# Two more parts of layer 0 in high and low halves, held in rings of four, with the parts placed mostly in tile 1 and the sum over d ahead of tile 1's half sum

## The reference, cut to what is computed

```python
e = jnp.stack([tbl_0[ids[:, 0]], ..., tbl_38[ids[:, 38]]], axis=1)      # (512, 39, 16)
x0 = xk = e
for W in (f0, f1, f2):                      # f0: (39*39, 128), f1 and f2: (128*39, 128)
    z = jnp.einsum('bfd,bgd->bfgd', x0, xk).reshape(b, f * g, d)
    cur = jnp.einsum('bpd,pm->bmd', z, W)
    outs.append(cur); xk = cur
z = jnp.sum(jnp.concatenate(outs, axis=1), axis=-1)                      # (512, 384)
h = relu(concat([z, dense_ctx]) @ W_top1 + b_top1)
h = relu(h @ W_top2 + b_top2)
y = h @ W_top3
```

## Time and profile before

| | us |
|---|---|
| median of 3 runs | 701.53 |
| the profiled execution | 700.51 |
| its span | 698.7 |
| around the span | 1.8 |

### The profile page before, as it was taken

The page is one execution under the profiler, slowest core; times in us unless marked ns, Lnnn a source line. Parts: engine busy times, 40 slices in busy tenths (PEclk is TensorE's granted clock), DMA queues, the critical chain, the costliest instruction groups (busy, mean ns, idle before and its releaser), DMA issues. The chain is left out here.

```text
span 698.7 us, 11739 instructions
## 1 busy us (share of the span) xinstructions
PE 643.2 (92%) x2567; PEld 472.3 (68%) x2567; DVE 538.7 (77%) x1216; ACT 518.5 (74%) x1842; POOL 429.9 (62%) x416
## 2 busy tenths in 40 slices
PE   0578999999999999999999999999999999999988
PEld 0246777676767677777777676767676777776663
DVE  1426788888887979797988888888979797999880
ACT  1226688788797878787887888787878787888862
POOL 6876568686767676767678686767676534101330
PEclk9877999999999999999999999999999999999999
DMA  7551332231304040313131221313040320301000
GB/s 206 117 118 30 88 74 45 45 72 37 80 10 106 9 107 3 85 31 77 39 77 40 56 61 39 77 23 93 9 108 4 96 63 0 109 0 44 29 1 0
DMA packets 58221, 40.28 MB, mean 58 GB/s; under 512 B 36626, under 2 KB 41056, under 8 KB 58203
## 3 DMA queue, kind: packets, MB, share of 16 engines
q1 hardware_dynamic: 52376, 38.73, 22.1%
q0 software_dynamic: 5120, 1.29, 2.4%
q10 hardware_dynamic: 706, 0.06, 0.1%
HBM read 38.13 MB, written 1.94 MB: 57 GB/s over the span
## 5 line engine op out<-in xcount | busy, mean ns | idle before, releaser
L640 ACT ACTIVATE parts<-psa,x0c 128x128 f32<-128x128 f32 x1536 | 440.7, 431 | 94.6 <-PE psa L793 88.2
L532 DVE SCALAR_TENSOR_TENSOR parts<-psd,x0c,parts 128x128 f32<-128x128 f32 x960 | 266.0, 342 | 80.9 <-PE psd L793 64.1
L503 DVE TENSOR_REDUCE cur<-parts 128x64 f32<-128x1536 f32 x128 | 223.6, 1747 | 23.7 <-ACT parts L640 18.8
L789 PE MATMUL psa<-w1h,x1h 128*128 128x512 f32 x384 | 175.3, 457 | 5.9 <-issue 5.9
L793 PE MATMUL psa<-w1h,x1l 128*128 128x512 f32 x384 | 152.4, 397 | 0.0
L790 PE MATMUL psa<-w1l,x1h 128*128 128x512 f32 x384 | 152.2, 396 | 0.0
L359 POOL TENSOR_TENSOR z0l<-pairs,z0h 117x512 fp32r<-117x512 f32 x56 | 72.7, 1298 | 122.6 <-ACT z0h L596 122.4
L343 POOL DMA_INDIRECT emb<-tables,idx x130 | 126.7, 975 | 23.3 <-issue 19.8
L352 POOL TENSOR_TENSOR pairs<-x0t,pairs 117x512 f32<-117x512 f32 (+1 forms) x105 | 135.1, 1296 | 7.3 <-DMA x0t<-x_rows 6.6
L789 PE MATMUL psd<-w1h,x1h 128*128 128x512 f32 (+1 forms) x256 | 115.2, 450 | 12.1 <-DVE parts L532 12.1
L793 PE MATMUL psd<-w1h,x1l 128*128 128x512 f32 (+1 forms) x256 | 97.8, 382 | 0.0
(11 more groups left out here) (83 smaller groups left out, 524.5 us busy)
## 6 DMA issues: line engine op xcount, KB each, us to landing
pairs<-x_rows SPq DMA_DIRECT2D x113, 156.0 KB
pairs<-x_rows SPq DMA_DIRECT2D x30, 234.0 KB
x0t<-x_rows SPq DMA_DIRECT2D x16, 234.0 KB
emb<-tables,idx POOLq DMA_INDIRECT x130
x_rows<-emb SPq DMA_DIRECT2D x13, 72.0 KB
wt_sb<-w_top SPq DMA_DIRECT2D x1, 768.0 KB, 5.9
parts<-w SPq DMA_DIRECT2D x1, 704.0 KB, 4.9
x_rows<-emb SPq DMA_DIRECT2D x13, 40.0 KB
```

The costliest lines, as they stand in the source:

```text
L503: return dve.tensor_reduce(cur1[:, t % 2, first:end], terms[:, first:end, :, :], AX.XY, ALU.add)
L532: op = dve.scalar_tensor_tensor(acc, y[:, M * j:M * j + M], x0c[:, t, GF * g + j:GF * g + j + 1], acc, ALU.mult, ALU.add)
L640: op = act.activation(lanes(dst, j), y[:, M * j:M * j + M], ACT.Copy, scale=x0c[:, t, GF * g + j:GF * g + j + 1])
L789: pe.matmul(y[:, 0:n], hi, w1h[:, c], start=True, stop=False)
```

## The change

Parts 0 and 1 join `SPLIT`, which is now 0 to 5; only part 6 stays in plain f32 and now closes the sum. `z0h` and `z0l` stay four slots large and become rings, so parts 4 and 5 take the slots of 0 and 1 once PE is through with these. The tables of all engines are new for every block but the first, and `SUM_AT` goes from tile 2 to the end of tile 1; `SCALARS_AT`, `ZH_AT` and `ZH_EARLY_AT` have no version of their own for block 0. POOL makes low parts 0 and 1 behind gather 8, and gather 9 goes ahead of low part 2.

```diff
-L0_AT = {(0, 5): 0, (0, 7): 1, (0, 9): 2, (1, 1): 3, (1, 3): 4, (1, 5): 6, (1, 8): 5}
-L0_AT_FIRST = {(1, 6): 0, (1, 8): 1, (2, 0): 2, (2, 2): 3, (2, 4): 4, (2, 6): 6, (2, 8): 5}
+L0_AT = {(0, 6): [0], (1, 0): [1], (1, 1): [2], (1, 3): [3], (1, 4): [4], (1, 8): [5], (1, 9): [6]}
+L0_AT_FIRST = {(1, 6): [0], (1, 8): [1], (2, 0): [2], (2, 2): [3], (2, 4): [4], (2, 6): [5], (2, 8): [6]}
...
-SPLIT = [2, 3, 4, 5]
-L0_END = 5
+SPLIT = [0, 1, 2, 3, 4, 5]
+L0_END = 6
 NS = len(SPLIT)
-ZH_AT = {(0, 2): 3, (0, 4): 4, (1, 1): 5}
-ZH_EARLY_AT = {(3, 4): 2}
+HIGHS, LOWS = 4, 4
+ZH_AT = {(0, 0): 3, (1, 0): 4, (1, 2): 5}
+ZH_EARLY_AT = {(2, 5): 0, (3, 0): 1, (3, 5): 2}
...
-SUM_AT, SUM_AT_FIRST = (2, 2), (3, 0)
-HIGH_AT = {(2, 4): 0, (3, 0): 1, (3, 2): 2}
+SUM_AT = (1, 3)
+SUM_AT_FIRST = (3, 0)
+HIGH_AT = {(2, 0): 0, (2, 3): 1, (3, 3): 2}
-LOW_AT = {(2, 3): 0, (3, 0): 1, (3, 1): 2}
+LOW_AT = {(2, 0): 0, (2, 3): 1, (3, 3): 2}
-SCALARS_AT = {(2, 2): 0, (2, 3): 1, (3, 1): 2}
+SCALARS_AT = {(1, 2): 0, (2, 0): 1, (3, 5): 2}
...
+        def high_slot(i):
+            return z0h[0:ROWS, COLS * (i % HIGHS):COLS * (i % HIGHS) + COLS]
...
                 pool.wait_ge(z0h_ready, (b - 2) * NS + i + 1)
+                pool.wait_ge(l0_steps, L0T * b + (SPLIT[i - LOWS] + 1 if i >= LOWS else 0))
...
                 if ahead2:
+                    pair_low_part(b + 2, 0)
+                    pair_low_part(b + 2, 1)
+                if gather_ahead:
+                    gather(9)
+                if ahead2:
                     pair_low_part(b + 2, 2)
-                if gather_ahead:
-                    gather(9)
...
-                act.wait_ge(l0_steps, L0T * b)
+                act.wait_ge(l0_steps, L0T * b + (SPLIT[i - HIGHS] + 1 if i >= HIGHS else 0))
...
-                    pe.matmul(ps0[:, :], w0h[0:ROWS, w], z0h[0:ROWS, c], start=False, stop=False)
+                    pe.matmul(ps0[:, :], w0h[0:ROWS, w], high_slot(i), start=(k == 0), stop=False)
```

More of the change, by code:

```diff
@@ L58 @@
 assert all(p.count("a") == SLOTS and p.count("d") <= SLOTS for p in PATTERN)
-L0_AT = {(0, 5): 0, (0, 7): 1, (0, 9): 2, (1, 1): 3, (1, 3): 4, (1, 5): 6, (1, 8): 5}
-L0_AT_FIRST = {(1, 6): 0, (1, 8): 1, (2, 0): 2, (2, 2): 3, (2, 4): 4, (2, 6): 6, (2, 8): 5}
-TURN_AT, TURN_AT_FIRST = (0, 8), (1, 5)
+L0_AT = {(0, 6): [0], (1, 0): [1], (1, 1): [2], (1, 3): [3], (1, 4): [4], (1, 8): [5], (1, 9): [6]}
+L0_AT_FIRST = {(1, 6): [0], (1, 8): [1], (2, 0): [2], (2, 2): [3], (2, 4): [4], (2, 6): [5], (2, 8): [6]}
+TURN_AT = (0, 8)
+TURN_AT_FIRST = (1, 5)
 WARMING = 3
-SPLIT = [2, 3, 4, 5]
-L0_END = 5
+SPLIT = [0, 1, 2, 3, 4, 5]
+L0_END = 6
 NS = len(SPLIT)
-ZH_AT = {(0, 2): 3, (0, 4): 4, (1, 1): 5}
-ZH_EARLY_AT = {(3, 4): 2}
+HIGHS, LOWS = 4, 4
+ZH_AT = {(0, 0): 3, (1, 0): 4, (1, 2): 5}
+ZH_EARLY_AT = {(2, 5): 0, (3, 0): 1, (3, 5): 2}
 assert sorted([*ZH_AT.values(), *ZH_EARLY_AT.values()]) == SPLIT
-SUM_AT, SUM_AT_FIRST = (2, 2), (3, 0)
-HIGH_AT = {(2, 4): 0, (3, 0): 1, (3, 2): 2}
+SUM_AT = (1, 3)
+SUM_AT_FIRST = (3, 0)
+HIGH_AT = {(2, 0): 0, (2, 3): 1, (3, 3): 2}
 HIGH_AT_FIRST = {(3, 2): 0, (3, 3): 1, (3, 5): 2}
-LOW_AT = {(2, 3): 0, (3, 0): 1, (3, 1): 2}
+LOW_AT = {(2, 0): 0, (2, 3): 1, (3, 3): 2}
 LOW_AT_FIRST = {(3, 1): 0, (3, 2): 1, (3, 3): 2}
-SCALARS_AT = {(2, 2): 0, (2, 3): 1, (3, 1): 2}
+SCALARS_AT = {(1, 2): 0, (2, 0): 1, (3, 5): 2}
 PIECES = [(0, 2), (2, 4), (4, L0T)]
@@ L148, in build @@
         pairs = sb("pairs", [128, L0T, COLS])
-        z0h = sb("z0h", [128, NS * COLS], F32R)
-        z0l = sb("z0l", [128, NS * COLS], F32R)
+        z0h = sb("z0h", [128, HIGHS * COLS], F32R)
+        z0l = sb("z0l", [128, LOWS * COLS], F32R)
         x1h = sb("x1h", [128, COLS], F32R)
@@ L172, in build, with low_slot @@
         y_sb = s0[0:1, :]
+        def high_slot(i):
+            return z0h[0:ROWS, COLS * (i % HIGHS):COLS * (i % HIGHS) + COLS]
+        def low_slot(i):
+            return z0l[0:ROWS, COLS * (i % LOWS):COLS * (i % LOWS) + COLS]
         def lanes(w, j):
@@ L357, in pair_low_part @@
                 pool.wait_ge(z0h_ready, (b - 2) * NS + i + 1)
-                c = slice(COLS * i, COLS * i + COLS)
-                pool.tensor_tensor(z0l[0:ROWS, c], pairs[0:ROWS, k, :], z0h[0:ROWS, c].bitcast(F32),
+                pool.wait_ge(l0_steps, L0T * b + (SPLIT[i - LOWS] + 1 if i >= LOWS else 0))
+                pool.tensor_tensor(low_slot(i), pairs[0:ROWS, k, :], high_slot(i).bitcast(F32),
                                    ALU.subtract).then_inc(z0l_ready, 1)
@@ L390, in first_block @@
                 gather_early(0, 9)
+                pair_low_part(2, 0)
+                pair_low_part(2, 1)
                 pair_low_part(2, 2)
@@ L438, in block_of @@
                 if ahead2:
-                    pair_low_part(b + 2, 2)
+                    pair_low_part(b + 2, 0)
+                    pair_low_part(b + 2, 1)
                 if gather_ahead:
                     gather(9)
+                if ahead2:
+                    pair_low_part(b + 2, 2)
             pool.wait_ge(ids_in, 16)
@@ L593, in pair_high_part @@
                 act.wait_ge(z0_ready, (b - 1) * L0T + k + 1)
-                act.wait_ge(l0_steps, L0T * b)
-                c = slice(COLS * i, COLS * i + COLS)
-                act.activation(z0h[0:ROWS, c], pairs[0:ROWS, k, :], ACT.Copy).then_inc(z0h_ready, 1)
+                act.wait_ge(l0_steps, L0T * b + (SPLIT[i - HIGHS] + 1 if i >= HIGHS else 0))
+                act.activation(high_slot(i), pairs[0:ROWS, k, :], ACT.Copy).then_inc(z0h_ready, 1)
             def high_part(b, t):
@@ L739, in layer0 @@
                     pe.wait_ge(z0l_ready, (b - 2) * NS + i + 1)
-                    c = slice(COLS * i, COLS * i + COLS)
                     w = slice(M * i, M * i + M)
-                    pe.matmul(ps0[:, :], w0h[0:ROWS, w], z0h[0:ROWS, c], start=False, stop=False)
-                    pe.matmul(ps0[:, :], w0h[0:ROWS, w], z0l[0:ROWS, c], start=False, stop=False)
-                    pe.matmul(ps0[:, :], w0l[0:ROWS, w], z0h[0:ROWS, c], start=False, stop=(k == L0_END)).then_inc(l0_steps, 1)
+                    pe.matmul(ps0[:, :], w0h[0:ROWS, w], high_slot(i), start=(k == 0), stop=False)
+                    pe.matmul(ps0[:, :], w0h[0:ROWS, w], low_slot(i), start=False, stop=False)
+                    pe.matmul(ps0[:, :], w0l[0:ROWS, w], high_slot(i), start=False, stop=(k == L0_END)).then_inc(l0_steps, 1)
                     return
@@ L795, in block_of @@
                             l0_at = L0_AT_FIRST if starts(b) else L0_AT
-                            if (t, g) in l0_at:
-                                layer0(b + 1, l0_at[t, g])
+                            for k in l0_at.get((t, g), []):
+                                layer0(b + 1, k)
                             if (t, g) == (TURN_AT_FIRST if starts(b) else TURN_AT):
@@ L809, in _ @@
             turn_x0(0)
-            for k in [*(k for k in range(L0T) if k != L0_END), L0_END]:
+            for k in range(L0T):
                 layer0(0, k)
```

## The result

The changed kernel takes 668.80 us, the median of four runs (666.62 to 670.97), against 701.25 of the kernel before in four runs on the same chip. The ratio is 0.9533, its interval 0.9494 to 0.9572, so 32.45 us are gone. The profiled execution took 669.16 us with a span of 667.3; in the two spans it is 31.4. Lines move: the groups of layer 1 are now L801, L802 and L805, the halves of a part L754 to L756, the part in f32 L759, the turn of x0 L770, `grams` L779, the half sum L517, the sum over d L511, x1l L507, DVE's products L546, ACT's products L653, x1h L624, the high part L609, the low part L368.

A forecast was written before the change was run, and what follows sets the result against it. PE was taken as the path, stalled by late DVE: A and B 18.6, C 9.1, parts 4.5, ends 0.9, less 1.0 residual stall, make 32.1 us; span 698.7 to 666.6, median 669.4, forecast 669, range 664 to 684.

The forecast's parts named there:

- A: PE's stall ahead of group 6 of tile 3, for a bank of DVE: 0.54 us a block, to go.
- B: PE's stall ahead of group 9 of tile 3, for a bank of DVE: 0.79 us a block, to go.
- C: PE's stall ahead of part 0 of the next block, for x1l: 0.70 us in 13 blocks, to go.
- The margins of 0.02 and 0.07: Time by which group 4's bank is free before group 9 needs it: 0.02 in tile 3, 0.07 in tile 2.
- ACT's idle 0.75: ACT's x1h of tile 0 waits 0.75 us for the sum over d, making DVE's half sum of tile 2 late.
- Parts, 0.16 each: Parts 0 and 1 in halves instead of f32 save PE 0.16 us each, 28 times: 4.5 us.
- The ends: Block 1's wait for x1l and block 15's stall: 0.9 us taken from both, between 0 and 2.
- Block 1's wait for x1l: PE's longest wait for x1l, 1.0 us, said to move a group back.
- The bound of 1.7 for block 0: In block 0 ACT may wait for the turn of x0 at (1, 2): nothing taken, 1.7 us at most.
- Rivals 2 and 3: POOL bounds: 690, chance 0.08; PE waits for z0l at (1, 4) and (1, 8): 715, chance 0.05.
- Rival 1: DVE stays late, so B stays at 0.3 to 1.0 us a block: 679, chance 0.19.
- Rival 4: Stalls only move to tile 2 or tile 0 and the parts alone are saved: 697, chance 0.06.

The follow-up runs named there:

- the DVE experiment: Changed kernel plus three sums over one input (tensor_reduce) on DVE behind the second half sum in tile 3: 672.34 us, ratio 0.972.
- the control: The changed kernel itself, unedited, run again on the third chip beside the third group of experiments: 660.41 us, ratio 0.9555.
- the first group: The first of three groups of follow-up runs, edits of the changed kernel; the kernel before took 700.62 us there.
- the other two groups: The second and third groups of follow-up runs, each on another chip; the kernel before took 691.93 and 691.17 us there.

## Why the prediction was right

It said 669, a gain of 32.1 and a block of 35.0; measured were 668.8, 32.4 (31.4 in the spans) and 35.04. That 669 was met to 0.2 is luck: the span came out 0.7 longer than the sum, and the median, put 1.0 above the profiled run, lay 0.4 below it; the two misses cancel. The block is the better test. Point by point:

- **PE is the path.** Right. Of the 37.30 us of the block before, 2.03 were A, B and C and 35.27 slots of matmuls; now PE is busy in all of a block, and each added stall of PE came out in the time: 0.50 in the DVE experiment made the block 0.50 longer.
- **A and B, 1.33 a block.** Right in size. The half sum of tile 2 was put at 0.64 into tile 3 and came at 0.71, the one of tile 3 at 0.83 into tile 0 and came at 1.04, its delay by ACT at 0.2 and was 0.25. The margins of 0.02 and 0.07 didn't hold fully, as foreseen: 0.07 of stall a block was allowed, and 0.10 is there, 0.05 in group 9 of tile 2 and of tile 3. The cause was told a little too simply: the prediction gives the delay as a chain through ACT's idle 0.75, but a late sum without that wait still costs 11.8 us of 17.3, 0.58 to 0.90 of a block's 1.14. The prediction has that term too ("so the sum (0.60) belongs where PE is slow"), but doesn't say how much it does; it is at least about as large as the wait.
- **C, 0.70 in 13 blocks.** Right, and it is the order that does it: C is absent with the sum late, too. But without the new order C would have grown to 0.93 through the halves, whose extra wait instructions the prediction had not priced. In the changed kernel part 0 begins 0.78 behind the end of x1l, more than the 0.45 that it needs, so they cost nothing there (C was to be gone by 1).
- **Parts, 0.16 each.** Near. By the blocks, two parts are worth 0.28 and a third 0.16 to 0.18. A slot of 512 columns is 0.233 at a granted clock of 1.00, and a part saves 0.14 to 0.18.
- **The ends.** Outside the twelve inner blocks the terms of the sum give 2 x 1.33 + 0.70 + 4 x 0.16 + 0.9 - 0.1 = 4.8, and 3.16 + 1.17 = 4.3 were measured. Inside they give 12 x 2.28 = 27.4 and 27.1 were measured. Block 1's wait for x1l, 1.04, did not vanish: it came back as 0.77 for a bank of DVE. The bound of 1.7 for block 0 was not called on.
- **POOL.** Right. Its block of 35.04 less 4.0 of waiting for ACT is a round of 31.0, put at 31.1. The waits stand where they were expected, 1.45 and 1.62 ahead of low parts 4 and 5, which begin 2.87 and 6.9 into tile 1 (put at 2.5 and 6.6), and 0.91 ahead of part 2's (put at 0.6). In this stretch POOL waits for no DMA. Its room of 4.0 us was then measured by loading it. Rivals 2 and 3 are off by that much, and they begin together.
- **Rival 1**, DVE late, did not come, but it was the nearest: 0.5 us more on DVE in tile 3 is at once 0.5 us of stall. Rival 4 is ruled out by the two tables of waits.

What stays open: how the cost of a late sum divides between ACT's wait and the sum's own time, and what delays the start of the kernel on the first chip (below).

## What to carry to other kernels

Stalls in several places of a loop can be one delay handed on from engine to engine; work them back, tile by tile, to the first instruction that is late, and check the sum of durations against each stall before using it forward. A busy engine can hide a small stall, here 0.05 us: look at the starts, and at the weight loads. Waits that had long been met still took some 0.1 us each in PE's queue here (0.19 for two), behind the wait that decided: count them where a release is on the path. Here half a microsecond on DVE, which had no room, came out in full in PE's time, so put such a step where the engine that sets the path is slow, and let that engine's extra work lie there too. Measure what an added load costs in its place, beside what then runs: a price taken from the same operation elsewhere was off by a fifth on POOL and by four times on DVE.

## What was not expected of the hardware

**DVE stands still behind POOL.** DVE's additions with two inputs from SBUF took 2071 to 2155 ns where they met POOL's subtractions, which have two inputs, eleven times in 42; the other 31 took 266 to 279, also beside a gather of POOL. Each of the eleven lasted until POOL was through with both of two subtractions in a row, and these were no longer than usual (1252 to 1318 ns over all 84). Operations with one input from SBUF in the same place, beside the same subtractions, took 261 to 268 (shortest, middle, longest of 42, in ns, from the groups of the timeline):

```profile
L559 DVE TENSOR_TENSOR probe<-ident_sb x42: 266/271/2155, 119.1 to 605.3; 117x117 f32<-117x117 f32 x42
```

```profile
L559 DVE TENSOR_REDUCE probe<-ident_sb x42: 261/265/268, 114.0 to 576.8; 117x1 f32<-117x117 f32 x42
```

The two loads differ in the operation as well as in the number of inputs, and no run separates these. The 28 subtractions that the change puts on POOL cost DVE nothing. DVE's products take one input from PSUM, and its half sums have one input: a product took 342 ns in the kernel before and 343 in the changed one, and a half sum takes the same 1.75 in both the earlier trace rows.

**The start differs between chips.** In the first profile ACT and DVE stand still early in block 0, and PE with them; in the control's they don't. The changed kernel in the two: the window of 10 us, in the first case with ACT's row.

```profile
43.00:53.00 10.00, 2.48 (x10) 1.38 (x8) 1.32 (x5) 0.00 (x0) 8.25 (x10) 0.82 0.56 127
```

```profile
53.33 1.15 ACT L653 ACTIVATE parts<-psa,x0c 128x128 f32<-128x128 f32 x4 [10.63 <-remote]
```

```profile
43.00:53.00 10.00, 10.00 (x47) 8.22 (x46) 8.32 (x23) 9.55 (x39) 8.21 (x11) 1.00 0.59 135
```

The turn of block 0 is at 63.11 in the first and at 52.16 in the second, 11 us apart, about the 9 to 10 us by which the kernel before differs as well. It is at 61.6 to 64.7 in the kernel before, the changed one and all four traces of the first group, and at 49.5 to 52.2 in all eight of the other two groups. The pauses themselves differ from kernel to kernel: in the kernel before (turn at 62.74) ACT stands still for 4.1 and for 3.1. What ACT waits for there the trace doesn't tell. Within the first group the turns differ by up to 3 us, and this can be in the differences of its times; the blocks from 2 on are free of it.
